# Moving the plain transfers of a fused two-layer graph network from SyncE's queue to GpSimd's

## The reference

```python
# layer 0: attention, 4 heads
h = relu(layernorm(x))
ht[head] = h @ W0[head]                       # 2048 x 256 per head
e = leaky_relu(src[:, None] + dst[None, :]) + adj
x1 = x + mean over heads of softmax(e, axis=-1) @ ht[head]
# layer 1: mean over neighbours
hidden = relu(layernorm(x1)) @ W1 + b1
A = (adj != 0);  deg = A.sum(axis=0)
out = x1 + (A @ hidden) / deg[:, None]
```

## Time and profile before

| | us |
|---|---|
| median of 3 runs | 619.67 (619.34 to 619.99) |
| the profiled execution, its own time | 619.52 |
| its span (first to last instruction) | 617.4 |
| TensorE busy | 531.0 (86%) |
| VectorE busy | 457.0 (74%) |
| ScalarE busy | 462.6 (75%) |
| GpSimd busy | 30.8 (5%) |

### The profile page before, as it was taken

The page is one execution under the profiler, slowest core; times in us unless marked ns, Lnnn a source line. Parts: engine busy times, 40 slices in busy tenths (PEclk is TensorE's granted clock), DMA queues, the critical chain, the costliest instruction groups (busy, mean ns, idle before and its releaser), DMA issues.

```text
span 617.4 us, 9010 instructions
## 1 busy us (share of the span) xinstructions
PE 531.0 (86%) x2991; PEld 303.0 (49%) x2991; DVE 457.0 (74%) x604; ACT 462.6 (75%) x391; POOL 30.8 (5%) x64
## 2 busy tenths in 40 slices
PE   6799569989898798989798898989798899777997
PEld 6333224545454454546454554544454455365885
DVE  5836665869678768878787888888778888263984
ACT  4647774979798878988898988888798886243861
POOL 4000000000000000000000000000000000000211
PEclk9879999989899989989999999999999999798999
DMA  8224151899999999999999999999999999941111
GB/s 321 62 102 184 35 102 35 153 225 179 227 225 206 217 188 213 206 213 206 221 223 209 226 203 230 200 221 193 219 230 206 227 198 201 233 131 58 43 42 42
DMA packets 300319, 108.91 MB, mean 176 GB/s; under 512 B 284748, under 2 KB 295372, under 8 KB 297724
## 3 DMA queue, kind: packets, MB, share of 16 engines
q1 hardware_dynamic: 300296, 108.62, 82.3%
HBM read 30.90 MB, written 6.39 MB: 60 GB/s over the span
## 4 chain that ended last, share of the span: by engine, by line
PE 27%; SPq 24%; ACT 15%; DMA 14%; issue 12%; DVE 7%; ACTq 0%; POOLq 0%; POOL 0%; DVEq 0%
SPq L296 12%; DMA probs_hi_t<-probs_hi 11%; PE ps_acc L736 11%; PE ps_relu L804 8%; SPq L304 7%; ACT logits L529 6%; ACT probs_hi L537 5%; SPq L314 3%; DVE logits L934 2%; ACT ps_relu L521 1%; PE ps_acc L714 1%; PE ps_h L714 1%; DMA x_all<-in_x 1%; DMA hidden_in<-hidden_scratch 1%; ACT x_all L452 1%
## 5 line engine op out<-in xcount | busy, mean ns | idle before, releaser
L736 PE MATMUL ps_acc<-h_w_split,probs_hi_t 128*128 128x512 f16 x1024 | 242.0, 391 | 48.7 <-DMA probs_hi_t<-probs_hi 47.3
L736 PEld LDWEIGHTS ps_acc<-h_w_split,probs_hi_t 128*128 128x128 f16 x1024 | 100.3, 100 | 171.2 <-DMA probs_hi_t<-probs_hi 54.2
L521 ACT ACTIVATE ps_relu<-dst_rows,src_bias 128x2048 f32<-128x2048 f32 x64 | 126.1, 1971 | 67.6 <-DVE small L934 67.4
L934 DVE CUSTOM_DVE_ANT_0 logits<-ps_relu,adj_rows 128x2048 f32<-128x2048 f32 x48 | 110.0, 2291 | 65.6 <-DMA adj_rows<-in_adj 33.8
L745 PE MATMUL ps_acc<-h_w_split,probs_lo_t 128*128 128x256 f16 x1024 | 122.7, 273 | 0.6 <-DMA probs_lo_t<-probs_lo 0.6
L943 DVE SCALAR_TENSOR_TENSOR probs_lo<-logits,small,probs_hi 128x2048 f16<-128x2048 f32 x48 | 112.7, 2349 | 0.3 <-ACT probs_hi L537 0.2
L745 PEld LDWEIGHTS ps_acc<-h_w_split,probs_lo_t 128*128 128x128 f16 x1024 | 96.3, 98 | 24.2 <-issue 10.4
L529 ACT ACTIVATE logits<-logits,small 128x2048 f32<-128x2048 f32 x48 | 95.4, 1988 | 0.0
L537 ACT ACTIVATE probs_hi<-logits,small 128x2048 f16<-128x2048 f32 x48 | 95.4, 1987 | 0.0
L804 PE MATMUL ps_relu<-hidden_split,mask_columns 128*128 128x512 f32 x256 | 62.9, 406 | 4.7 <-DVE hidden_split L1032 4.2
L804 PEld LDWEIGHTS ps_relu<-hidden_split,mask_columns 128*128 128x128 f32 x256 | 49.7, 195 | 16.6 <-DVE hidden_split L1032 4.8
(11 more groups left out here) (93 smaller groups left out, 380.4 us busy)
## 6 DMA issues: line engine op xcount, KB each, us to landing
adj_rows<-in_adj SPq DMA_DIRECT2D x16, 1024.0 KB, 6.1
dst_rows<-dst_scratch SPq DMA_DIRECT2D x3, 1024.0 KB, 6.3
x_all<-in_x SPq DMA_DIRECT2D x4, 512.0 KB, 6.1
x<-in_x SPq DMA_DIRECT2D x16, 128.0 KB, 2.5
x_scratch<-x SPq DMA_DIRECT2D x16, 128.0 KB, 1.9
hidden_scratch<-hidden SPq DMA_DIRECT2D x16, 128.0 KB, 2.2
out<-out_rows SPq DMA_DIRECT2D x16, 128.0 KB, 1.7
x_in<-x_scratch SPq DMA_DIRECT2D x1, 1792.0 KB, 8.1
```

The source lines that it names most:

```text
L521: nc.scalar.activation(R[:, :], D[:, h, :], ACT.Relu, scale=(1.0 - SLOPE) / SLOPE, bias=src[:, bass.ds(u, 1)]).then_inc(relu_ready, 1)
L736: last = nc.tensor.matmul(ACC[parity][:, :], TA[:, e, b, :], H[:, h, b, :], start=(h == 0 and b == 0), stop=False)
L934: nc.vector.tensor_tensor_reduce(out=logits_of(h, parity), in0=R[:, :], in1=ADJ[:, parity, :], scale=-1.0, scalar=3.0e38, op0=ALU.add, op1 ...
```

## The change

The load of `adj` for blocks 1 to 15, the load of the residual, both scratch stores and the reloads of `hidden` are issued by GpSimd, in a list of its own, with the same semaphores and the same conditions. SP keeps the loads ahead of the attention, all transposes, the two reloads of `x1` and the stores of the output. GpSimd's list for block ib is: store `x1(ib-1)`, `rstd_of(ib-1)`, store `hidden(ib-2)`, load `adj(ib+2)`, load the residual of ib. The adjacency of block 0, which SP still loads, gets a semaphore of its own (`adj0_in`). The removed helper functions (from `store_hidden` to `load_adj`) stand in the added lines again, with the other engine's name.

```diff
--- before.py
+++ after.py
@@ -165,7 +165,7 @@
         x_in = [sem(f"x_in{g}") for g in range(4)]
         w0_in, a0_in, w1_in, b1_in = sem("w0_in"), sem("a0_in"), sem("w1_in"), sem("b1_in")
-        adj_in, xres_in = [sem("adj_in0"), sem("adj_in1")], sem("xres_in")
+        adj0_in, adj_in, xres_in = sem("adj0_in"), [sem("adj_in0"), sem("adj_in1")], sem("xres_in")
         x1_stored, hid_stored = sem("x1_stored"), sem("hid_stored")
         hid_in = [sem(f"hid_in{n}") for n in range(4)]
         x1_in, out_stored = [sem("x1_in0"), sem("x1_in1")], [sem("out_stored0"), sem("out_stored1")]
@@ -252,40 +252,13 @@
             sp.dma_start(WR[:, :, :], w0.rearrange("(k p) d -> p k d", p=P)).then_inc(w0_in, 16)
             sp.dma_start(AB[:, :, :].rearrange("p h d -> p (h d)"),
                          a0.rearrange("h d o -> (h d o)").partition_broadcast(P)).then_inc(a0_in, 16)
-            sp.dma_start(ADJ[:, 0, :], adj[0:P, :]).then_inc(adj_in[0], 16)
+            sp.dma_start(ADJ[:, 0, :], adj[0:P, :]).then_inc(adj0_in, 16)
             sp.dma_start(W1[:, :, :], w1.rearrange("(k p) f -> p k f", p=P)).then_inc(w1_in, 16)
             sp.dma_start(B1[:, :], b1.partition_broadcast(P)).then_inc(b1_in, 16)
             def passed(b):
                 if not isinstance(b, int):
                     sp.sem_inc(passed_sp, 1)
-
...
             def transpose_hi(u, e):
                 sp.wait_ge(probs_hi_ready, u + 1)
@@ -314,34 +287,14 @@
                 sp.dma_start_transpose(mask_slot(b).bitcast(u16).rearrange("p (c i) -> p c i", c=CH),
                                        rows.bitcast(u16)).then_inc(mask_in, 16)
-            def load_hidden(n):
-                lo, hi = PARTS[n]
-                sp.wait_ge(hid_stored, 32 * hi)
-                sp.dma_start(HIN[:, lo:hi, :, :], paired(hid_dram)[:, lo:hi, :, :]).then_inc(hid_in[n], 16)
-
             def slot(ib, h, parity):
                 u = 4 * ib + h
                 if has(u + 2):
                     transpose_hi(u + 2, h % 2)
-                if h == 1 and past(ib, 2):
-                    store_hidden(ib - 2)
-                if h == 1 and past(ib, 1):
-                    store_x1(ib - 1)
-                if h == 3:
-                    load_residual(ib)
                 if has(u + 2):
                     transpose_lo(u + 2, h % 2)
-                if h == 2 and not (isinstance(ib, int) and ib + 2 >= NB):
-                    load_adj(ib + 2, parity)
                 if h == 3 and not final(ib):
                     transpose_mask(ib + 1)
-                if final(ib) and h == 0:
-                    sp.wait_ge(probs_lo_ready, UNITS - 4)
-                    sp.wait_ge(mask_in, 16 * NB)
-                    load_hidden(0)
-                if final(ib) and h == 2:
-                    sp.wait_ge(probs_lo_ready, UNITS)
-                    load_hidden(1)
             transpose_mask(0)
@@ -357,7 +310,6 @@
             sp.wait_ge(w_lo_ready, 1)
             for h in range(1, HEADS):
                 sp.dma_start(D[:, h, :], dst_dram[0, h, :].partition_broadcast(P)).then_inc(dst_in[h], 16)
-            load_adj(1, 1)
             transpose_hi(0, 0)
             transpose_lo(0, 0)
             transpose_hi(1, 1)
@@ -368,14 +320,9 @@
                     slot(ib, h, parity)
             block_loop(sp, body)
-            load_hidden(2)
-            store_hidden(NB - 2)
             sp.wait_ge(unit_multiplied, UNITS - 3)
             sp.wait_ge(x1_stored, 16 * (NB - 2))
             sp.dma_start(X1R[:, 0:CH - 1, :, :], paired(x1_dram)[:, 0:CH - 1, :, :]).then_inc(x1_in[0], 16)
-            store_x1(NB - 1)
-            store_hidden(NB - 1)
-            load_hidden(3)
             sp.wait_ge(x1_stored, 16 * NB)
             sp.dma_start(X1R[:, CH - 1:CH, :, :], paired(x1_dram)[:, CH - 1:CH, :, :]).then_inc(x1_in[1], 16)
@@ -408,17 +355,73 @@
                 pool.wait_ge(x_veps_ready, g + 1)
                 nc.gpsimd.tensor_tensor(RS[:, c], VE[:, c], power[:, :], ALU.pow).then_inc(x_rstd_ready, 1)
+            def passed(b):
+                if not isinstance(b, int):
+                    pool.sem_inc(passed_pool, 1)
+
+            def store_hidden(b):
+                pool.wait_ge(hid_ready, b + 1)
+                passed(b)
+                nc.gpsimd.dma_start(hid_dram[bass.ds(b * P, P), :], HID[:, :]).then_inc(hid_stored, 16)
+
+            def store_x1(b):
+                pool.wait_ge(x1_ready, b + 1)
+                passed(b)
+                nc.gpsimd.dma_start(x1_dram[bass.ds(b * P, P), :], X1[:, :]).then_inc(x1_stored, 16)
+
+            def load_residual(b):
+                if past(b, 1):
+                    pool.wait_ge(norm1_ready, b)
+                    passed(b)
+                    pool.wait_ge(x1_stored, 16 * b)
+                    passed(b)
+                nc.gpsimd.dma_start(X1[:, :], x[bass.ds(b * P, P), :]).then_inc(xres_in, 16)
+
+            def load_adj(ib, parity):
+
+                if isinstance(ib, int) and ib == 1:
+                    pool.wait_ge(pieces_ready, 1)
+                else:
+                    pool.wait_ge(probs_lo_ready, 4 * ib - 4)
+                    passed(ib)
+                nc.gpsimd.dma_start(ADJ[:, parity, :], adj[bass.ds(ib * P, P), :]).then_inc(adj_in[parity], 16)
+
+            def load_hidden(n):
+                lo, hi = PARTS[n]
+                pool.wait_ge(hid_stored, 32 * hi)
+                nc.gpsimd.dma_start(HIN[:, lo:hi, :, :], paired(hid_dram)[:, lo:hi, :, :]).then_inc(hid_in[n], 16)
+
             def rstd_of(b):
                 pool.wait_ge(mv_ready, b + 1)
-                pool.sem_inc(passed_pool, 1)
+                passed(b)
                 nc.gpsimd.tensor_scalar(veps[:, :], mv[:, 1:2], EPS, None, ALU.add).then_inc(veps_ready, 1)
                 pool.wait_ge(veps_ready, b + 1)
-                pool.sem_inc(passed_pool, 1)
+                passed(b)
                 nc.gpsimd.tensor_tensor(rstd[:, :], veps[:, :], power[:, 0:1], ALU.pow).then_inc(rstd_ready, 1)
-            rstd_of(0)
-            with pool.Fori(1, NB) as b:
-                rstd_of(b)
+            def body(ib, parity):
+                if past(ib, 1):
+                    store_x1(ib - 1)
+                    rstd_of(ib - 1)
+                if past(ib, 2):
+                    store_hidden(ib - 2)
+                if not (isinstance(ib, int) and ib + 2 >= NB):
+                    load_adj(ib + 2, parity)
+                load_residual(ib)
+
+            load_adj(1, 1)
+            block_loop(pool, body)
+            pool.wait_ge(probs_lo_ready, UNITS - 4)
+            pool.wait_ge(mask_in, 16 * NB)
+            load_hidden(0)
+            pool.wait_ge(probs_lo_ready, UNITS)
+            load_hidden(1)
+            load_hidden(2)
+            store_hidden(NB - 2)
+            store_x1(NB - 1)
+            rstd_of(NB - 1)
+            store_hidden(NB - 1)
+            load_hidden(3)
             def half_x1(c, t, j):
@@ -843,8 +846,14 @@
                 nc.vector.scalar_tensor_tensor(MB[:, c], MV[:, c, 0], -1.0, RS[:, c], ALU.mult, ALU.mult)\
                     .then_inc(x_bias_ready, 1)
+            def adj_there(ib, parity):
+                if isinstance(ib, int) and ib == 0:
+                    vec.wait_ge(adj0_in, 16)
+                else:
+                    vec.wait_ge(adj_in[parity], 8 * (ib + parity))
+
             def mask_rows(ib, parity):
-                vec.wait_ge(adj_in[parity], 8 * (ib - parity) + 16)
+                adj_there(ib, parity)
                 last = isinstance(ib, int) and ib == NB - 1
                 if last:
                     vec.wait_ge(probs_lo_ready, UNITS - 4)
```

22 lines of the change are left out of this document (removed).

## The result

The changed kernel takes 654 us where the kernel before takes 619.5: the ratio of the runs is 1.056, with a 95% interval of 1.052 to 1.060. The four runs of the changed kernel are 651.1, 656.8, 663.6 and 668.1 us; the two longest are disturbed and are left out of the ratio and of the 654, and the profile shown here is that of the third. Its time is 663.64, its span 661.9 us. The forecast was 596, with a range to 622.

A forecast was written before the change was run, and what follows sets the result against it. SP's always-issuing queue was taken to hold blocks at 27.5 us, above floors of 22.9 to 24.5. From 619.5 us, 25 saved in the attention and 1 lost in the tail gave 595.5, say 596; range 582 to 622.

The forecast's parts named there:

- the 3.0 us of freed issue time: SP's queue: issue time per block of the adj load, residual load and two stores, removed from SP.
- D: Delay of the high transpose behind the adj load, per block: 2.1 us, with bounds 0 and 5.6.
- TensorE's 23.9: TensorE's floor per block: its four units' work without waits, 23.9 us.
- The latency loop: Transpose, TensorE, VectorE, ScalarE back to the transpose three units on: 17.16 us, or 22.9 a block.
- B: Length of one attention block in us: 27.5 before, forecast 25.8 after the change.
- Rows overtake transposes: Rival, chance 0.15: on two queues the load's 8 KB rows delay transposes in flight; slower, 633 us.
- Its deciding point, D = 5.1: Delay of the high transpose from which the overtaking rival was said to decide: 5.1 us.
- If a piece is served for each row: Overtaking rival's mechanism in the DMA engines: transposes stand still or lose their rate as the load's rows take turns.
- The DMA engines are the bound: Rival, chance 0.17: only a quarter of the freed issue time is usable, 0.75 us a block; 609.5 us.
- the wait moves: Rival, chance 0.06: the load holds both transposes up, delay 5 us; 1 us saved in all, 619.5 us.
- The tail: Behind the last block: reloads, stores and clock together 1 us lost, between -4 and +5.
- the 25 us of gain: Attention: 1.7 us saved a block, counted over 14.5 blocks, 25 us.

The follow-up runs named there:

- e9: The kernel before without the small transfers' DMAs in the ten looped blocks (semaphores only raised, output not the reference's): 612.3 us, ratio 0.989.
- e1: The changed kernel with the load of adj back on SP at its old place, small transfers still on GpSimd: 628.0 us, ratio 1.012.
- e2: The changed kernel with the load of adj back on SP, one unit earlier than its old place: 639.7 us, ratio 1.035.
- e4: The changed kernel with GpSimd's load of adj split into four column quarters (2 KB rows): 660.0 us, ratio 1.063.
- e13: The kernel before with the load of adj issued by ScalarE's queue at the change's early moment: 617.6 us, ratio 0.995.
- e11: The kernel before with the load of adj alone moved to GpSimd, at the change's early moment: 636.1 us, ratio 1.027.
- e18: e17 with twelve needless multiplications on TensorE ahead of its wait for the high transpose behind the load: 634.5 us, ratio 1.025.
- e16: The changed kernel with two small powers on GpSimd delaying the load of adj, in the first four blocks only: 635.7 us, ratio 1.025.
- e17: The changed kernel with four small powers on GpSimd ahead of the load of adj in every block: 656.6 us, ratio 1.059.
- e3: The changed kernel with GpSimd's load of adj held one unit later, to about the old moment: 635.4 us, ratio 1.028.
- e7: The kernel before with SP's load of adj in front of the low transpose instead of behind it: 615.8 us, ratio 0.995.

## Why the prediction was wrong

**"SP hardly ever waits for anybody, which means that it is always issuing, and whatever stands in its list is issued late."** This step failed first. The reading of the earlier trace rows was right, and SP did begin to wait after the change (41.2 us, more than the 3 us a block that I gave). But the 3.0 us of freed issue time were priced as if SP set the pace. `e9` frees 2.0 of them, and 1 us of data with them, and gains 0.7 us a block. `e1`, with the small transfers alone taken from SP, loses 0.9 us a block.

**"Low transpose (0.52 MB at 217 GB/s, 2.4 us) and load end by 310.92 + 2.4 + 2.8 = 316.1, so that high transpose starts D = 2.1 us late."** This step turned the sign. It let the low transpose go first and pass free, and put the delay on the high one alone. On the chip the low one landed 3.9 us late, the high one 3.3 us late. The low transpose's multiplication has next to no slack: 3.14 of the 3.9 us become waiting, and they add to TensorE's 23.9 directly, which makes 27.0. The three later periods of the change in which the granted clock stays at 1.00 are 27.2, 27.4 and 28.0; with the others, where it falls behind the wait, the mean is 28.5. This path explains the later blocks of the change, but it is not the only one that leads there: `e1` has 28.4 without it, with its waits for `adj` and for high transposes as before (24.8 and 26.3 us). The bound of 5.6 for D was drawn too narrow as well: in four blocks the low transpose was 9 to 13 us late. These blocks are the largest piece of the error, 27 us, and the sum had no term for them.

**"The latency loop has slack 0.75 B - 17.2."** Too generous by 1.5 us in one unit of four. In `e2` the high transpose behind the load is late by 2.95 us, and the three units it ends, from the high multiplication at 415.08 us to that at 436.73, take 21.65 us, not 17.16 + 2.95 = 20.1. Its timeline shows why: TensorE has seeded by 419.03, and VectorE comes to the logits only at 420.49, behind the sums and statistics of `x1`.

```profile
418.63 0.40 PE L727 MATMUL ps_relu<-dst_pieces,pick_rows 12*128 12x512 bf16 x4
...
420.49 2.29 DVE L943 CUSTOM_DVE_ANT_0 logits<-ps_relu,adj_rows 128x2048 f32<-128x2048 f32 x1 [0.16 <-issue]
```

**"Rows overtake transposes"**, with 0.15, was the right rival by its direction and by its late transposes, and its price of 633 us was too low by 21. Its deciding point, D = 5.1, was wrong, since the delay fell on the low transposes, where any microsecond counts. "If a piece is served for each row": `e4` fits it and does not prove it. Against the rival I had "today's load delays its neighbour by only about its own length"; that row was of one queue, and `e13`, and one load of `e11`, show that it still holds with a second queue when the load enters with the transpose. It was no evidence on a load that enters later. The Trainium skill (DMA: Bandwidth & Descriptors, Issuing engines are not separate DMA queues) says that more issuing engines save only the usually small issue time. That there is little to gain agrees with `e9`. It is not all that a second issuer changed here: the load on GpSimd costs 1.4 to 2.7% by itself.

**"The DMA engines are the bound"** and **"the wait moves"**: the strip did not rise, and the attention moves 207 GB/s in the kernel before and 204 in `e18`, at shares of 1.03 and 1.02. If the DMA engines are near their limit there, that may be why freed issue time buys so little; no run here takes data away without taking issues away too, so that stays open.

**What was right.** VectorE's wait for `adj` is gone; the high transpose with 5 us to issue is no longer at h = 3 but at h = 2, beside the load (5.12 us at 313.94); the 3.61 us before the last high multiplication are 1.16. GpSimd's issue was taken at 1.0 us and takes 0.54 to 0.64, at most 0.95; it is hidden. Of all this nothing shortened the kernel. One number of my text was misread: for the last high multiplication I wrote a granted clock of 0.50, and the row of that stretch has 0.55.

**The tail.** I had it at 1 us lost, up to 5. The stages behind the attention are 8.9 us longer in the one profile. The named mechanism is there, the reloads of `hidden` issued from 565.17 on behind the last residual load, and the aggregation that waits for them (all engines, from 560 us on):

```profile
565.17 2.07 POOL L392 DMA_DIRECT2D hidden_in<-hidden_scratch  x3
...
574.85 3.28 PE L748 MATMUL ps_acc<-h_w_split,probs_lo_t 128*128 128x256 f16 x16 [4.12 <-DMA probs_lo_t<-probs_lo]
574.89 1.48 ACT L589 ACTIVATE hidden_split<-hidden_in 128x1536 fp32r<-128x1536 f32 x1 [20.28 <-DMA hidden_in<-hidden_scratch]
```

GpSimd's three reloads (1792 KB together) beside SP's last low transpose, which lands in 10.5 us and makes TensorE wait for 4.12, look like the loop's collision once more.

**Sum.** Against 596: the 25 us of gain did not come, the later blocks lost some 8, the first four 27, and the tail up to 8 instead of 1. 25 + 8 + 27 + 8 makes 68 us, and the profiled execution is 67.6 above the forecast; the 654 us of the ratio are 58 above it. Shown is that a delay of the load mends the four bad blocks (`e16`), and that the clock adds to the wait (`e17` against `e18`). Not shown is what happens inside the DMA engines: why GpSimd's load and a transpose end together, and why an entry 0.27 us behind the start of an issue is so much worse in the change than one at 0.7, and not in `e3`. Even at 2.0 to 2.2 us the unrolled blocks are worse than the looped ones (4.8 to 7.3 against 4.3), so the distance is not the whole of it.

## What to carry to other kernels

A queue that never waits is full, but only a run that takes issues away from it tells what its time is worth; here 2 us of it were worth 0.7. Read the blocks one by one: four of thirteen periods held most of the loss, and a mean hides that. Before a bulk load is moved to another engine's queue, ask which transfer it will then lie beside, and price a delay of each one in flight, not only of the one behind: the one whose consumer has no slack decides. And where a load must be somewhere, try its place on its old queue first (`e7`, 0.5% from two swapped lines), in front of the transfer that has the most slack.

## What the runs showed that I had not expected

- A GpSimd load of 1024 KB and an SP transpose in flight end together in the block shown, the transpose in 8.4 us instead of 4.5, and the transpose lands in 13.3 to 17.9 us in the four blocks of the change where the load entered 0.27 us after its issue began; the DMA engines then show full shares at 122 GB/s over ten microseconds.
- The same load on ScalarE's queue, issued within 0.04 us of the transpose, lands in 5.7 us, and the transpose takes 5.52 us to issue, as behind a load on SP's own queue; one load of `e11` on GpSimd's queue, 0.02 us behind a transpose, did the same (5.5 and 5.33 us).
- In `e1` even 128 KB on GpSimd's queue land in 4.3 to 4.5 us, where SP's took 1.8 to 2.5; in the change the same ones land in 2.1 to 3.9.
- Waits of TensorE of 3.1 and 3.9 us are followed by the 1.2 GHz level (matmuls of 3.59 us instead of 1.92, and 6.44 instead of 3.62), while waits of 3.25 to 3.51 us in `e2` are not; with 2.84 us of needless multiplications in front, the wait of 1.28 us that is left is not either, and 22 us of the stage come back.
